# In the last hop TensorE turns the identity forty times a batch into an unused part of PSUM

## The chip, the cores and the metric

One core of one Trainium2 chip runs the kernel. The metric is the time on the device in microseconds, of the one core; lower is better.

## The reference

Two graph layers over 50,000 nodes of 128 features and 25,000 edges, each followed by a layer norm:

```python
x = layernorm(x + L0(x, (src, dst), edge_attr_70, Wf, bf, Wq, Wk, Wa, Wu, bu))
x = layernorm(x + L1(x, edge_attr3_4x1, src, dst))

# L0, per edge:  f = elu(concat(x[src], x[dst], x[src]-x[dst], attr) @ Wf + bf) * mask
#                a = tanh((x[src] @ Wq) * (f @ Wk) * scale @ Wa)
#                z = exp(a) / exp(segment_sum(a, src))[src] * f
#     result:    (x + segment_sum(z, src)) @ Wu + bu
# L1: e2 = e / segment_sum(e, dst)[dst] over the edges in both directions, self edges weigh 0
def f(y): return segment_sum(y[src3] * e3, dst3)       # four heads of 32 features
k1 = f(x); k2 = f(x + k1/3); k3 = f(x + k2 - k1/3); k4 = f(x + k1 - k2 + k3)
y = x + (k1 + 3*(k2 + k3) + k4) / 8
```

The second layer is linear in `f`, so the kernel applies `f` four times in a row ("four hops") and adds the results with the shares 1, 1/2, 1/6 and 1/24.

## The kernel before

The kernel sorts the 50,000 ends of edges by node, so that each of 128 partitions holds a run of 392 rows (`C`), worked in 49 batches (`NB`) of 8 rows (`B`). It has three parts, and each engine has its own program in each of them.

1. The edges' messages (0 to about 740 us), with the sort on VectorE.
2. The first layer's second pass (about 765 to 1450 us): GpSimd gathers message rows, VectorE sums runs and makes the norm's statistics, TensorE turns rows through the identity (line 831) and multiplies with `Wu` (lines 818 and 822).
3. The four hops (`hop(h)`, h = 0 to 3). For each batch GpSimd issues eight indirect gathers (line 1319); VectorE weighs the rows (`weigh`, line 1433, which raises `z_set`), adds the value carried over from the last row (`go_on`, 1444), sums runs with a scan in PSUM (`add_up_runs`, 1452), keeps the last row (`keep_last`, 1458, which raises `last_kept`) and divides (`divide`, 1462). ScalarE lays out the scan's pattern (1371) and scales the rows for the running total (1388), VectorE adds them (1417). SyncE moves totals and rows between HBM and SBUF.

In the hops 0 to 2 the nodes without edges are worked beside it: TensorE multiplies 384 of their rows a batch (`d_tensor`, line 1100), VectorE adds and makes statistics (`d_res_set` counts its additions), ScalarE scales.

The last hop (h = 3) also makes the output: VectorE adds the first layer's row to the total (`o_rows`, line 1185), takes the statistics with eight `bn_stats` (1189) and, after a wait on its own semaphore `o_stat`, eight `bn_aggr` (1193); ScalarE takes the root (`o_root`, 1161 and 1163) and scales eight rows (`o_scale`, 1170); GpSimd stores them with eight indirect DMAs (`o_put`, 1200). GpSimd's order there is: the gathers of batch b, then the stores of batch b - 4, which wait for `o_normed`. TensorE has nothing in the last hop's 49 batches. After the last batch it makes one product (`carry`, line 1353), which waits for `last_kept`; VectorE's `cross` (line 1527) waits for it, then `cross_sum` (1533), then the last batch's shift, which ScalarE's last `o_scale` and GpSimd's last eight stores need.

In PSUM the hops use banks 0 and 1 for the weighed rows (`z_all`), banks 2 to 4 for the weights (`wt`), bank 7 for the scaled rows (`shared`), columns 0 to 127 of bank 6 for the carry, and columns 128 to 511 of banks 5 and 6 for the dense products of the hops 0 to 2 (`d_new_psum`). In the last hop nothing uses bank 5.

Of the kernel before, what the change touches and what calls it, by code (L numbers as in the profile page):

```python
# [59 lines left out]
DC = N // 128 // DR  # L60
DMAIN = DC * DR * 128
DREST = N - DMAIN
DSLOTS = 44


def sort_before(k):
# [21 lines left out]
def build(nc, x, src, dst, e_in, Wf, bf, Wa, Wu, bu, x_t, ea_t, ea_0, wqk_in, out):  # L88
# [10 lines left out]
    with ExitStack() as ctx:  # L99
        def sb(name, shape, dt=F32, stage=None):  # L100
            return (stage or ctx).enter_context(nc.sbuf_tensor(name, shape, dt))
# [5 lines left out]
        bank = [psum[:, i * 512:(i + 1) * 512] for i in range(8)]  # L107

        ident = sb("ident", [128, 128])
# [949 lines left out]
        def d_landed(k):  # L1059
            return attr_count(NS - 1 - (NS - 1 - k) % 4) + times(k, 4) * 16  # L1060
# [6 lines left out]
        def d_shape(k):  # L1067
            return (DREST, 1) if k == DC else (128, DR)
# [14 lines left out]
        def d_store(sp, k):  # L1083
            if 0 <= k <= DC:
                P, RR = d_shape(k)
                sp.wait_ge(d_normed_set, k + 1)
                sp.dma_start(d_rows(out, k), d_normed[k % 4][0:P, 0:RR, :]).then_inc(d_out[k % 4], 16)

        def d_tensor(pe, k):
            if k > DC:  # L1090
                return
            P, RR = d_shape(k)
            if k == 0:
                pe.wait_ge(f_norm, 1)
                pe.wait_ge(wu_i_set, 1)
            pe.wait_ge(attr_in[k % 4], d_landed(k))
            if k >= 2:
                pe.wait_ge(d_res_set, k - 1)
            for r in range(RR):
                t = pe.matmul(d_new_psum[k % 2][0:P, r * D:(r + 1) * D], d_xt[k % 4][:, r * 128:r * 128 + P], wu_i[:, :],  # L1100
                              start=True, stop=True)
            t.then_inc(d_mm, 1)
# [115 lines left out]
        def hop(h):  # L1218
# [6 lines left out]
            def dense_at(b):  # L1225
                if h < 3 and 1 <= b <= (DC + 5 - 2 * DSLOTS if h == 2 else DSLOTS):
                    return h * DSLOTS + b - 1
                return None

            done = h * NB  # L1230
# [29 lines left out]
            def hop_sync(sp):  # L1260
# [5 lines left out]
                for b in range(NB + 1):  # L1266
# [13 lines left out]
                    if dense_at(b) is not None:  # L1280
                        d_store(sp, dense_at(b) - 5)
                    if h == 2 and b == DC + 6 - 2 * DSLOTS:
                        d_store(sp, DC)
# [64 lines left out]
            def hop_tensor(pe):  # L1348
                for b in range(NB):
                    if dense_at(b) is not None:  # L1350
                        d_tensor(pe, dense_at(b))
                pe.wait_ge(last_kept, (h + 1) * NPC)
                pe.matmul(carry, chain[:, :], last_z[:, 0:D], start=True, stop=True).then_inc(carried, 1)  # L1353

# [51 lines left out]
            def hop_vector(v):  # L1406
# [135 lines left out]
                if h == 3:  # L1542
# [11 lines left out]
                                           ).then_inc(f_norm, 1)  # L1554

            return hop_sync, hop_gpsimd, hop_tensor, hop_scalar, hop_vector

        hops = [hop(h) for h in range(4)]
# [69 lines left out]
```

## Time and profile before

| | |
|---|---|
| time, median of 3 runs | 4298.1 us (4269.28 to 4321.41) |
| the profiled execution's own time | 4300.45 us |
| its span in the trace | 4298.3 us |
| VectorE busy | 2368.8 us (55%), 6013 instructions |
| GpSimd busy | 2656.3 us (62%), 2760 instructions |
| ScalarE busy | 1326.2 us (31%) |
| TensorE busy | 879.6 us (20%), 3855 instructions |
| mean granted clock of TensorE | 0.575 of full speed |

An engine's busy time counts its instructions, not the time between them. For GpSimd that matters: each of its indirect DMAs is followed by about 0.3 us in which it issues the next one, and this time isn't in the 62%.

### The profile page before, as it was taken

How to read it: one execution, taken by the hardware profiler on the slowest of the kernel's cores; microseconds unless marked ns; L12 is line 12 of the kernel's file. 1: busy time of each engine (PE TensorE's matmuls, PEld its weight loads, DVE VectorE, ACT ScalarE, POOL GpSimd, SP SyncE). 2: the span in 40 equal slices, each digit the busy share in tenths (PEclk: the TensorE clock that was granted, in tenths of full speed). 3: DMA queues.
4: the chain of work that ended last, by engine and by line, in shares of the span. 5: the costliest groups of instructions: out<-in, count | busy, mean ns of one | idle time of the engine just before them, and what ended most of it. 6: DMA issues, size and time to landing. Idle time of an engine off the chain costs nothing.

```text
span 4298.3 us, 23047 instructions
## 1 busy us (share of the span) xinstructions
PE 879.6 (20%) x3855; PEld 697.7 (16%) x3855; DVE 2368.8 (55%) x6013; ACT 1326.2 (31%) x3061; POOL 2656.3 (62%) x2760
## 2 busy tenths in 40 slices
PE   2443545354555311110111110111100000000000
PEld 2443434133333201110011110111100000000000
DVE  5445441466666745665567765666765434443443
ACT  2332334254555312221233331333322222222222
POOL 5555553655555466665666656666657677666766
PEclk7776768677776655555555555555555555555555
DMA  4343337454555334443566665566653333332332
GB/s 88 115 130 109 128 104 147 131 161 156 158 161 157 113 104 126 128 134 117 173 217 224 223 209 177 194 226 211 226 181 127 111 97 113 110 101 92 127 98 86
DMA packets 272344, 621.66 MB, mean 145 GB/s; under 512 B 100374, under 2 KB 137199, under 8 KB 265945
## 3 DMA queue, kind: packets, MB, share of 16 engines
q1 hardware_dynamic: 176754, 421.49, 28.9%
q0 software_dynamic: 94672, 198.33, 17.0%
q14 instruction: 119, 0.97, 0.1%
q8 instruction: 31, 0.51, 0.0%
q10 hardware_dynamic: 768, 0.36, 0.0%
HBM read 318.61 MB, written 310.84 MB: 146 GB/s over the span
## 4 chain that ended last, share of the span: by engine, by line
DVE 26%; another core or an unknown queue 21%; issue 17%; POOL 10%; ACT 5%; PE 2%; DMA 1%; DVEq 0%; ACTq 0%; POOLq 0%
DVE psum L1452 8%; POOL gs L1319 5%; POOL out_dram L1200 4%; DVE da L1462 4%; PE psum L822 2%; ACT psum L1388 2%; DVE stats L933 2%; DVE psum L958 1%; DVE psum L1433 1%; DVE da L966 1%; DVE tn L1417 1%; DVE d_stats L1143 1%; DVE new_res L929 1%; DVE d_res L1138 1%
## 5 line engine op out<-in xcount | busy, mean ns | idle before, releaser
L1319 POOL DMA_INDIRECT gs<-u,far_row x1176 | 1120.5, 953 | 486.0 <-issue 347.6
L1388 ACT ACTIVATE psum<-da 128x512 f32<-128x512 f32 x288 | 173.2, 601 | 1612.7 <-remote 676.9
L318 POOL DMA_INDIRECT pt<-in_x_dram,idx x392 | 382.6, 976 | 321.7 <-DMA rows_e<-pt 198.8
L800 POOL DMA_INDIRECT gs<-rows_e,edge_id x392 | 371.6, 948 | 326.2 <-DVE new_res L929 155.8
L1200 POOL DMA_INDIRECT out_dram<-normed,out_idx x392 | 396.5, 1012 | 211.3 <-issue 115.5
L1100 PE MATMUL psum<-wu_i,d_xt 128*128 128x128 f32 (+1 forms) x782 | 211.0, 443 | 1421.9 <-DVE d_res L1138 501.7
L1319 POOL DMA_INDIRECT gs<-x1s,far_row x392 | 373.3, 952 | 175.7 <-issue 128.1
L1452 DVE TENSOR_TENSOR_SCAN psum<-goes_on,psum 128x1024 f32<-128x1024 f32 (+1 forms) x200 | 449.4, 2247 | 42.9 <-remote 23.7
L1100 PEld LDWEIGHTS psum<-wu_i,d_xt 128*128 128x128 f32 (+1 forms) x782 | 176.4, 326 | 1456.2 <-issue 1456.2
L1433 DVE TENSOR_TENSOR psum<-gs,psum 128x1024 f32<-128x1024 f32 x192 | 233.1, 1214 | 270.5 <-DMA gs<-u,far_row 228.4
L1417 DVE TENSOR_TENSOR tn<-psum,gs 128x512 f32<-128x512 f32 x288 | 197.7, 686 | 109.2 <-issue 66.5
L1353 PE MATMUL psum<-last_z,chain 128*128 128x128 f32 x8 | 3.2, 501 | 1173.0 <-issue 1073.8
L1462 DVE TENSOR_TENSOR da<-psum,inv 128x1024 f32<-128x1024 f32 (+1 forms) x200 | 238.6, 1193 | 0.3
L360 PE MATMUL psum<-w_src,xs_t 128*128 128x256 f32 x392 | 164.6, 511 | 348.9 <-ACT xd_t L390 277.0
L1371 ACT COPY goes_on<-cont_in 128x1024 f32<-128x1024 f32 (+1 forms) x200 | 201.9, 1011 | 68.1 <-DVE psum L1452 32.2
L1444 DVE SCALAR_TENSOR_TENSOR psum<-last_z,cont,psum 128x128 f32<-128x128 f32 x196 | 68.9, 352 | 271.8 <-remote 193.0
L664 DVE SCALAR_TENSOR_TENSOR act_f<-psum,ex 128x512 f32<-128x512 f32 x49 | 33.8, 690 | 334.6 <-ACT ex L440 202.1
L1353 PEld LDWEIGHTS psum<-last_z,chain 128*128 128x128 f32 x8 | 2.0, 311 | 1174.3 <-issue 1074.1
L822 PE MATMUL psum<-wu,rows_t 128*128 128x128 f32 x784 | 143.5, 357 | 222.9 <-ACT rows_t L886 160.8
L822 PEld LDWEIGHTS psum<-wu,rows_t 128*128 128x128 f32 x784 | 131.3, 261 | 278.0 <-ACT rows_t L886 205.3
L911 ACT ACTIVATE normed<-new_res,shift,rstd 128x128 f32<-128x128 f32 x392 | 156.2, 482 | 54.5 <-DVE shift L979 44.1
L929 DVE TENSOR_TENSOR new_res<-gs,psum 128x1024 f32<-128x1024 f32 (+1 forms) x50 | 60.0, 1199 | 190.9 <-PE psum L822 127.7
(223 smaller groups left out, 3036.1 us busy)
## 6 DMA issues: line engine op xcount, KB each, us to landing
u<-da SPq DMA_DIRECT2D x144, 512.0 KB
rows_e<-pt SPq DMA_DIRECT2D x48, 1056.0 KB
total<-tn SPq DMA_DIRECT2D x98, 512.0 KB
gs<-total SPq DMA_DIRECT2D x98, 512.0 KB
gs<-u SPq DMA_DIRECT2D x49, 512.0 KB
gs<-x1s SPq DMA_DIRECT2D x49, 512.0 KB
res_d<-new_res SPq DMA_DIRECT2D x49, 512.0 KB
d_xt<-x_t_dram SPq DMA_DIRECT2D x130, 192.0 KB
```

The source lines that it names most:

```text
L318: g.indirect_dma_start(pt[i][:, j, r, FX:FX + D], None, x[:, :], bass.IndirectOffsetOnAxis(ap=idx[:, r, s, j:j + 1], axis=0)).then_inc(x_i ...
L800: g.indirect_dma_start(gs[b % NG][:, j, :], None, rows_e[:, :], bass.IndirectOffsetOnAxis(ap=edge_id[:, c:c + 1], axis=0)).then_inc(x_in[b ...
L822: t = pe.matmul(new_psum[:, j * D:(j + 1) * D], xa_t[b % 2][:, j * 128:(j + 1) * 128], wu[:, :], start=False, stop=(j % 4 == 3))
L1100: t = pe.matmul(d_new_psum[k % 2][0:P, r * D:(r + 1) * D], d_xt[k % 4][:, r * 128:r * 128 + P], wu_i[:, :], start=True, stop=True)
L1200: g.indirect_dma_start(out[:, :], bass.IndirectOffsetOnAxis(ap=out_idx[:, c:c + 1], axis=0), normed[k % 3][:, j, :], None, bounds_check=bo ...
L1319: g.indirect_dma_start(gx[b % 4][:, j * D:(j + 1) * D], None, source[:, :], bass.IndirectOffsetOnAxis(ap=far_row[:, c:c + 1], axis=0)).the ...
L1371: act.copy(goes_on[i % 2][:, 0:n * D].rearrange("p (f j) -> p f j", j=n), cont_in[:, b * B + c0:b * B + c1].unsqueeze(1).to_broadcast([128 ...
L1388: act.mul(shared, half(us[b % 3], i), share).then_inc(shared_set, 1)
L1417: v.tensor_tensor(half(tn[b % 3][:, :, :], i), shared, half(tp[b % 3], i), ALU.add).then_inc(tn_set, 1)
L1433: return v.tensor_tensor(zf.rearrange("p (h f) j -> p j h f", h=H), by_head(gxv(b % 4)[:, c0:c1, 0:D]), per_head(wt_rest[:, c0:c1, :] if b ...
L1452: v.tensor_tensor_scan(z, goes_on[i % 2][:, 0:(c1 - c0) * D], z, 0.0, ALU.mult, ALU.add).then_inc(run_set, 1)
L1462: return v.tensor_tensor(by_head(us[b % 3][:, c0:c1, :]), zf.rearrange("p (h f) j -> p j h f", h=H), per_head(inv[:, b * B + c0:b * B + c1 ...
```

## The change

A constant `WARM` of 40, and six lines in TensorE's program for a hop. In the last hop, before the first batch, TensorE waits until VectorE has read the last dense product out of PSUM. Then, for each of the 49 batches, it waits until the batch's weighing product is done (`z_set`) and turns the 128x128 identity through itself forty times into columns 128 to 255 of bank 5. The carry's product stays behind the last of them in TensorE's queue. Nothing reads what is written, and no other engine's program changes.

```diff
--- before.py
+++ after.py
@@ -61,6 +61,7 @@
 DMAIN = DC * DR * 128
 DREST = N - DMAIN
 DSLOTS = 44
+WARM = 40
 
 
 def sort_before(k):
@@ -1349,6 +1350,12 @@
                 for b in range(NB):
                     if dense_at(b) is not None:
                         d_tensor(pe, dense_at(b))
+                    if h == 3:
+                        if b == 0:
+                            pe.wait_ge(d_res_set, DC + 1)
+                        pe.wait_ge(z_set, done + b + 1)
+                        for i in range(WARM):
+                            pe.transpose(bank[5][:, 128:256], ident[:, :], ident[:, :])
                 pe.wait_ge(last_kept, (h + 1) * NPC)
                 pe.matmul(carry, chain[:, :], last_z[:, 0:D], start=True, stop=True).then_inc(carried, 1)
```

## Rows read from the trace of the kernel before

**Rows 1.** Profile page: TensorE's busy tenths and granted clock in 40 slices, instruction queues

```profile
PE   2443545354555311110111110111100000000000
...
PEclk7776768677776655555555555555555555555555
...
q8 instruction: 31, 0.51, 0.0%
```

**Rows 2.** Windows: third and last hop; busy us (count) per engine, clock, DMA share, GB/s

```profile
2640.00:3188.00 548.00, 67.89 (x250) 56.36 (x250) 365.46 (x682) 170.99 (x365) 343.84 (x363) 0.50 0.63 207
3188.00:4298.30 1110.30, 0.80 (x2) 0.50 (x2) 493.65 (x1235) 273.04 (x637) 777.28 (x786) 0.50 0.33 108
```

**Rows 3.** Groups by line in the last hop: count, busy us, mean ns, idle before

```profile
L1200 POOL DMA_INDIRECT out_dram<-normed,out_idx x392 | 396.5, 1012 | 211.3 <-issue 115.5 <-ACT normed L1170 95.8
L1319 POOL DMA_INDIRECT gs<-u,far_row x392 | 378.8, 966 | 121.9 <-issue 118.9 <-DMA u<-cross,first_idx 2.7 <-remote 0.3
...
L1452 DVE TENSOR_TENSOR_SCAN psum<-goes_on,psum 128x1024 f32<-128x1024 f32 x48 | 109.8, 2288 | 10.9 <-remote 10.1 <-issue 0.8
...
L1193 DVE BATCH_NORM_AGGREGATE mv<-stats 128x2 f32<-128x6 f32 x392 | 33.8, 155 | 168.1 <-remote 120.3 <-issue 45.8
```

**Rows 4.** Timeline of one late stretch: start us, us, engine, line, count, idle before

```profile
3638.91 1.22 DVE L1185 SCALAR_TENSOR_TENSOR new_res<-gs,tn 128x1024 f32<-128x1024 f32 x1
...
3643.09 0.32 SPq L1279 DMA_DIRECT2D res_d<-new_res  x1
3643.09 1.65 DVE L1189 BATCH_NORM_STATS2 stats<-new_res 128x6 f32<-128x128 f32 x8 [2.96 <-remote]
...
3653.59 0.86 DVE L1193 BATCH_NORM_AGGREGATE mv<-stats 128x2 f32<-128x6 f32 x8 [8.86 <-issue]
...
3671.31 1.02 POOL L1200 DMA_INDIRECT out_dram<-normed,out_idx  x1 [6.17 <-ACT normed L1170]
```

**Rows 5.** Groups by line in the first layer's second pass, 820 to 1440 us

```profile
L800 POOL DMA_INDIRECT gs<-rows_e,edge_id x346 | 328.0, 948 | 257.9 <-DVE new_res L929 155.8 <-issue 102.1
...
L958 DVE TENSOR_TENSOR_SCAN psum<-goes_on,psum 128x1024 f32<-128x1024 f32 x45 | 103.3, 2295 | 39.0 <-remote 28.1 <-issue 8.0 <-DVE psum L954 2.0
...
L937 DVE BATCH_NORM_AGGREGATE mv<-stats 128x2 f32<-128x6 f32 x380 | 30.5, 153 | 1.7
```

**Rows 6.** Line 831 (turns through the identity): ns min/median/max, all its instructions

```profile
L831 PE MATMUL psum<-ident,da x392: 272/273/476, 772.0 to 1433.1; 128*128 128x128 f32 x196
```

**Rows 7.** Timeline of TensorE: eight turns of line 831, twice

```profile
1108.13 1.39 PE L831 MATMUL psum<-ident,da 128*128 128x128 f32 x8
...
1117.19 1.09 PE L831 MATMUL psum<-ident,da 128*128 128x128 f32 x8 [1.50 <-DVE da L966]
```

**Rows 8.** Timeline of the third hop: three dense products

```profile
2719.08 1.62 PE L1100 MATMUL psum<-wu_i,d_xt 128*128 128x128 f32 x6 [18.69 <-issue]
```

**Rows 9.** Groups by line in the third hop: the dense products

```profile
L1100 PE MATMUL psum<-wu_i,d_xt 128*128 128x128 f32 x246 | 66.4, 443 | 424.4 <-issue 182.9 <-DVE d_res L1138 131.8 <-remote 109.7
```

**Rows 10.** Timeline of the end: last product, carry, what waits for it, last stores

```profile
4247.77 0.70 DVE L1433 TENSOR_TENSOR psum<-gs,wt_rest 128x512 f32<-128x512 f32 x1
...
4254.87 0.29 DVE L1458 COPY last_z<-psum 128x128 f32<-128x128 f32 x1 [0.49 <-DVE psum L1452]
...
4255.59 0.80 PE L1353 MATMUL psum<-last_z,chain 128*128 128x128 f32 x2 [1073.84 <-issue]
...
4266.88 0.26 DVE L1527 TENSOR_TENSOR cross<-psum,inv_first 128x128 f32<-128x128 f32 x1
...
4275.19 3.19 ACT L1170 ACTIVATE normed<-new_res,shift,rstd 128x128 f32<-128x128 f32 x8 [0.59 <-remote]
...
4285.22 0.98 POOL L1200 DMA_INDIRECT out_dram<-normed,out_idx  x1 [0.31 <-issue]
...
4295.53 0.98 POOL L1342 DMA_INDIRECT out_dram<-new,fix_idx  x1 [0.30 <-issue]
```

## The prediction

> **What bounds the kernel now.** I read the page first, then windows by hop, then the groups by line in the last hop, then single stretches of the timeline. On the page TensorE's row is zero over the last quarter, and its granted clock stands at 0.5, the lower of its two levels (1.2 GHz), from about 1460 us to the end [rows 1]. The windows make the last hop 1110.3 us long, with VectorE busy 493.7 us, ScalarE 273.0 us, GpSimd 777.3 us, and the DMA engines at a third [rows 2]. None of these is full, but the groups by line show that GpSimd is the bound: its stores take 396.5 us and its gathers 378.8 us, between them lie 115.5 + 118.9 us in which it only issues the next one, and it waits 95.8 us for ScalarE's scaled rows and 3.0 us for other things. That is 396.5 + 378.8 + 115.5 + 118.9 + 95.8 + 3.0 = 1108.5 of the 1110.3 us [rows 2, 3]. So the last hop gets shorter only if the 95.8 us shrink or each indirect DMA gets cheaper, and longer if GpSimd waits more.
>
> Where do the 95.8 us come from? VectorE's eight bn_aggr, which need nothing but the eight bn_stats before them, sit idle 168.1 us in front of them over the hop [rows 3]. The timeline shows such a stretch. An addition ends at 3638.91 + 1.22 = 3640.13 us, yet both the statistics behind it on VectorE and SyncE's store of its result start only at 3643.09 us; then the first bn_aggr comes 8.86 us after the last bn_stats, and at 3671.31 us GpSimd has lost 6.17 us [rows 4]. I call this VectorE's lag: its completions are seen late. In the first layer's second pass the same pair of instructions has 1.7 us of idle time over 380 bn_aggr [rows 5]. That pass differs from the last hop in two ways. TensorE works there, with its clock often at the upper level (tenths 7 and 8 on the page) [rows 1]. And GpSimd rests: 155.8 us in waits for VectorE within 620 us [rows 5]. The trace of before can't part these two, and this is the main doubt of the forecast.
>
> **The change, part by part.** Nothing is removed or moved. Added in the last hop are:
>
> 1. One wait for the last dense addition. That addition belongs to the third hop, so the wait is over before the last hop has products. Cost nothing.
> 2. 49 waits on `z_set` in TensorE's program, and 49 x 40 = 1960 turns. Eight turns of line 831 take 1.09 us at best, the last of them being 0.27 us long, so the step is (1.09 - 0.27) / 7 = 0.117 us; another eight took 1.39 us, (1.39 - 0.27) / 7 = 0.16 us [rows 6, 7]. At the low clock no row has turns alone; the nearest are dense products in the third hop, six records in 1.62 us, one of them 0.443 us long, a step of (1.62 - 0.443) / 5 = 0.236 us [rows 8, 9]. I take a burst of forty between 40 x 0.117 = 4.7 us and 40 x 0.236 = 9.4 us, nearer 8 us, because TensorE has idled before each burst. If no turn overlapped the next, at the longest turn of 0.476 us, it would be 19.0 us [rows 6]. A batch lasts 1110.3 / 49 = 22.7 us [rows 2]. So a burst fits into its batch in each of these cases, TensorE is done before the next `z_set`, and the clock should rise within bursts. The work lies beside GpSimd's and costs nothing.
> 3. Instructions to fetch. The queue that I take for TensorE's, from its size of 0.51 MB for 3855 matmul and 3855 load records (66 bytes each), had 31 transfers [rows 1]. The change adds 3920, so 0.26 MB or 16 transfers, against 108 GB/s x 1110 us = 120 MB in the hop [rows 2]. Below: nothing. Above, if each stood in front of a gather for 1 us (an assumption; a gather instruction itself takes 0.97 us [rows 3]): 16 us. I take nothing, since gathers are issued up to three batches ahead.
> 4. The carry's product, which is now behind the last burst. The last product ends at 4247.77 + 0.70 = 4248.47 us. The burst then ends at 4248.5 + 9.4 = 4257.9 us, the carry 0.80 us later, at 4258.7 us instead of 4256.39 us. VectorE comes to `cross` only at 4266.88 us, so 8.2 us of cover remain; without that cover the cost would be 2.3 us. With 19.0 us for the burst the carry ends at 4268.3 us, 1.4 us after `cross` now starts. Behind it lies more cover: the last eight rows are scaled by 4275.19 + 3.19 = 4278.38 us and GpSimd stores them from 4285.22 us on, 6.8 us later [rows 10]. Cost nothing in both.
>
> Other engines' durations: does a working TensorE change them? VectorE's scan takes 2295 ns in the pass in which TensorE works and 2288 ns in the last hop, where it doesn't [rows 3, 5], and a gather 948 ns against 966 ns. So no row shows an instruction that gets slower or faster by more than 2% with TensorE's work beside it. The Trainium skill ("SBUF — State Buffer", section "Who interferes with whom") says that TensorE has SBUF ports of its own and that contention arises only at the pair that VectorE and GpSimd share. By that rule too the bursts cost nothing.
>
> Sum: 0 us against the profiled execution's 4300.45 us, which is 2.4 us above the median of 4298.1 us. I forecast 4298 us.
>
> **The rivals.**
>
> *VectorE's lag goes away (faster).* If that lag hangs on TensorE's idleness, as the comparison of the two stages allows, the bursts would make the last hop like the second pass, in which the pair has 1.7 us of idle time. GpSimd then no longer waits for scaled rows: at most 4300.45 - 95.8 = 4204.7 us, half of it 4252.6 us [rows 3, 5]. Against it: the dense products of the third hop keep TensorE busy 67.9 of 548 us [rows 2], and the pauses of GpSimd explain the clean stage as well. The Trainium skill ("TensorE: Matmul & The Clock Gate", section "Seeing it yourself") states that only TensorE has this clock gate, with none for VectorE. By that rule the raised clock gives the other engines nothing, and the sum stays at 4300; no run so far shows it.
>
> *VectorE's lag gets worse (slower).* In the last hop, between a product and the next, VectorE's completions are late already. If what delays them is a resource that all engines' instructions share, 80 more records a batch lengthen the lag. Each microsecond that it adds to GpSimd's wait is lost in full. Were the wait to double, the time is 4300.45 + 95.8 = 4396 us; from 43 us more on, an increase by 45%, the change is slower by 1% [rows 3]. Against it: the second pass runs TensorE, VectorE, ScalarE and GpSimd together with next to none of it [rows 5].
>
> *TensorE can't keep the pace.* From 22.7 / 40 = 0.57 us a turn on TensorE is the bound and the carry is late. At 0.70 us a burst takes 28 us, and 49 of them 1372 us, 262 us more than the hop, 4562 us. Against it: the longest of 392 turns took 0.476 us [rows 6].
>
> *The change doesn't do what it says:* the clock stays at 0.5. That costs and gains nothing, since bursts of 9.4 us are in the sum above. It shares the forecast's time.
>
> **How the numbers follow.** No change within 1%: 0.62, own range 4265 to 4330 us, about the spread of the three runs. Lag relieved: 0.22. Lag worse: 0.14. TensorE the bound: 0.02. One per cent is about what a measurement of this kernel can tell from no change. Of the relief's 0.22 I count 0.19 as more than 1%, and 0.02 of chance spread, so faster 0.21; slower 0.14 x 0.8 + 0.02 + 0.02 of spread = 0.15; the rest is 0.64. The range goes down to 4225 us, which leaves out the nearly full relief (about 0.10), and up to 4335 us, which leaves out about 0.09 of the slower cases.
>
> **What would show each step.** In the profile of after: 1960 turns at the new line with a burst of 5 to 9 us in each batch; the clock's row above 0.5 in the last quarter; GpSimd's wait for scaled rows still near 96 us, and the idle time before bn_aggr near 168 us; the carry's product later by 1 to 3 us with `cross` where it was. If the wait for scaled rows falls below 50 us, TensorE's idleness was the cause and I am wrong. If it rises above 140 us, the bursts stand in VectorE's way.

## The result, and the profile after

The changed kernel takes 4403.7 us (median of 4 runs, 4388.9 to 4414.4) beside 4304.8 us for the kernel before (4269.3 to 4321.4): a ratio of 1.022, 95% interval 1.018 to 1.026. That is outside the range given. The profiled execution took 4405.02 us, its span is 4403.2 us, 104.9 us more than the span before.

The page of the changed kernel, same rows as [rows 1] and TensorE's total:

```profile
PE 1211.6 (28%) x5815; PEld 955.4 (22%) x5815; DVE 2370.5 (54%) x6013; ACT 1326.3 (30%) x3061; POOL 2650.8 (60%) x2760
...
PE   2544433444455111110111101111032122211237
...
PEclk7777767677777555555555555555555555555568
...
q8 instruction: 46, 0.75, 0.1%
```

TensorE is at 1 to 3 tenths over the last quarter and at 7 only in the last slice. The clock's row stays at 0.5, the lower level (1.2 GHz), until the last two slices. So the turns are there, but thinly spread.

Groups by line in the last hop (count, busy us, mean ns, idle before and what ended it). The first two and the last answer to [rows 3]; line numbers are seven or fewer higher than before:

```profile
L1201 POOL DMA_INDIRECT out_dram<-normed,out_idx x392 | 395.9, 1010 | 311.2 <-ACT normed L1171 195.7 <-issue 115.5
L1320 POOL DMA_INDIRECT gs<-u,far_row x392 | 378.4, 965 | 121.9 <-issue 119.1 <-DMA u<-cross,first_idx 2.8
L1358 PE MATMUL psum<-ident 128*128 128x128 f32 x1960 | 354.5, 313 | 843.4 <-issue 823.1 <-DVE psum L1440 19.9
...
L1459 DVE TENSOR_TENSOR_SCAN psum<-goes_on,psum 128x1024 f32<-128x1024 f32 x48 | 109.9, 2289 | 10.6 <-remote 5.4 <-issue 4.7
```

GpSimd's own work is that of before, to within a microsecond. Its wait for scaled rows has gone from 95.8 to 195.7 us. And the 1960 turns have 843.4 us of idle time in front of them. 823.1 us of it end with nothing that the profile shows ("issue"), and only 19.9 us with the weighing product. The waits in the same stretch (engine, tile, line waited for: us in total, times, longest us):

```profile
POOL out_dram L1201 <- ACT normed L1171: 195.7, 13, 86.5
DVE mv L1194 <- remote: 152.9, 19, 9.6
...
DVE cross L1534 <- PE psum L1360: 103.1, 2, 102.8
ACT normed L1171 <- DVE shift L1177: 99.9, 1, 99.9
```

One single wait is 86.5 us long, so it makes most of the difference: VectorE's `cross` waits 102.8 us for the carry's product, the last shift comes behind it, and GpSimd's last eight stores behind that. The timeline shows how it comes about, first TensorE some 90 us into the hop (start us, us, engine, line, operation, count, idle before):

```profile
3285.45 0.37 PE L1358 MATMUL psum<-ident 128*128 128x128 f32 x1 [1.79 <-issue]
3288.26 0.37 PE L1358 MATMUL psum<-ident 128*128 128x128 f32 x1 [2.45 <-issue]
3291.07 0.37 PE L1358 MATMUL psum<-ident 128*128 128x128 f32 x1 [2.43 <-issue]
```

then a stretch in which GpSimd waits for scaled rows:

```profile
3249.78 14.76 PE L1358 MATMUL psum<-ident 128*128 128x128 f32 x110 [0.34 <-issue]
...
3256.10 1.02 POOL L1201 DMA_INDIRECT out_dram<-normed,out_idx  x1 [11.33 <-ACT normed L1171]
```

and the end, TensorE and GpSimd:

```profile
4302.65 0.98 POOL L1201 DMA_INDIRECT out_dram<-normed,out_idx  x1 [0.30 <-issue]
...
4306.28 79.44 PE L1358 MATMUL psum<-ident 128*128 128x128 f32 x711 [1.03 <-issue]
4385.56 0.39 PE L1360 MATMUL psum<-last_z,chain 128*128 128x128 f32 x2
...
4385.99 0.29 DVE L1534 TENSOR_TENSOR cross<-psum,inv_first 128x128 f32<-128x128 f32 x1 [102.78 <-PE psum L1360]
...
4390.18 1.00 POOL L1201 DMA_INDIRECT out_dram<-normed,out_idx  x1 [86.55 <-ACT normed L1171]
```

While GpSimd issues without a pause, a turn lasts 0.37 us and the next comes up to 2.80 us later. When GpSimd waits, TensorE catches up: GpSimd stands still from 3244.77 to 3256.10 us, and from 3249.78 us on 110 turns go in 14.76 us, 0.134 us each. Behind the first 53 turns the hop has ten such blocks, of 22 to 110 turns; each begins within one of the twelve waits for scaled rows that GpSimd has before its last. They hold 712 of the 1249 turns made until GpSimd stops, in 101.5 us; the 484 others take about 2.0 us each on average. When GpSimd issues its last store but eight, at 4302.65 us, more than 711 of the 1960 turns are undone, some 18 batches' worth. Some 2.7 us after that store has been issued, TensorE starts on these 711 and does them in 79.44 us, 0.112 us each, and only then comes the carry.

The sum of the difference: the hop starts 6.1 us later (its first gather at 3194.21 instead of 3188.10 us; up to there the two programs do the same, and in the traces of the experiments on such chips this gather starts anywhere from 3168.9 to 3213.8 us), the other waits for scaled rows grow from 95.8 to 195.7 - 86.5 = 109.2 us, 13.4 us more, and the late carry costs 86.5 us. Together that is 106.0 us, beside the 104.9 us of the two spans.

### The profile page after: what moved, and what is told of

Read it like the earlier page. It is cut to its first block, busy times and chain, and to the rows that moved or that the text cites. A ratio compares the mean times of both kernels' runs of the same rounds, so it can differ in the third digit from the quotient of the medians.

```text
span 4403.2 us, 26968 instructions
## 1 busy us (share of the span) xinstructions
PE 1211.6 (28%) x5815; PEld 955.4 (22%) x5815; DVE 2370.5 (54%) x6013; ACT 1326.3 (30%) x3061; POOL 2650.8 (60%) x2760
## 4 chain that ended last, share of the span: by engine, by line
issue 31%; DVE 24%; another core or an unknown queue 11%; PE 10%; POOL 3%; ACT 2%; DMA 1%; DVEq 0%; ACTq 0%; POOLq 0%
PE psum L1358 8%; DVE psum L1459 7%; DVE da L1469 4%; POOL gs L1320 2%; PE psum L823 2%; DVE psum L959 2%; DVE da L967 1%; DVE d_stats L1144 1%; DVE stats L934 1%; DVE psum L1440 1%; DVE tn L1424 1%; DVE new_res L930 1%; ACT psum L1395 1%; DVE d_res L1139 1%
## 5 line engine op out<-in xcount | busy, mean ns | idle before, releaser
L1358 PE MATMUL psum<-ident 128*128 128x128 f32 x1960 | 354.5, 313 | 843.4 <-issue 823.1
L1201 POOL DMA_INDIRECT out_dram<-normed,out_idx x392 | 395.9, 1010 | 311.2 <-ACT normed L1171 195.7
L1358 PEld LDWEIGHTS psum<-ident 128*128 128x128 f32 x1960 | 269.5, 161 | 928.5 <-issue 928.3
L1378 ACT COPY goes_on<-cont_in 128x1024 f32<-128x1024 f32 (+1 forms) x200 | 201.9, 1012 | 76.6 <-DVE psum L1459 50.8
L1171 ACT ACTIVATE normed<-new_res,shift,rstd 128x128 f32<-128x128 f32 x392 | 155.4, 479 | 99.9 <-DVE shift L1177 99.9
L912 ACT ACTIVATE normed<-new_res,shift,rstd 128x128 f32<-128x128 f32 x392 | 156.3, 482 | 50.5 <-DVE shift L980 47.7
```

The source lines that it names most:

```text
L1201: g.indirect_dma_start(out[:, :], bass.IndirectOffsetOnAxis(ap=out_idx[:, c:c + 1], axis=0), normed[k % 3][:, j, :], None, bounds_check=bo ...
L1358: pe.transpose(bank[5][:, 128:256], ident[:, :], ident[:, :])
```

## The experiments

**What was to be told apart.** Theory A: TensorE falls behind because each turn has to wait for something that all engines share while GpSimd issues without a pause; the forty turns a batch pile up and the carry is late. Rival B: the turns make VectorE's lag (its late completions) worse throughout the hop. Rival C: it is TensorE's own busy time, or the clock that follows from it.

### Turns in the first 28 batches only

```diff
-                    if h == 3:
+                    if h == 3 and b < 28:
```

> The forty turns stand only in the last hop's first 28 batches. Theory A, TensorE falls behind: in the changed kernel it has done about 31 bursts (1240 turns) when GpSimd stops at about 4300 us, so it gets through a turn in about 1090 / 1240 = 0.88 us while the hop runs. 28 bursts are 1120 turns, 985 us, done by 4192 us, before the last product; the carry's product is on time and the time is that of the kernel before, ratio 1.000 (within 1%). Theory B, the turns lengthen VectorE's lag and so GpSimd's waits all along the hop: 28 of 49 bursts keep 28/49 of the 99 us, about +57 us, ratio 1.013.

Measured: 4316.2 us, ratio 1.0028 (0.9995 to 1.0061). `cross` waits 0.3 us for TensorE, GpSimd 107.5 us for scaled rows, none of it over 11.4 us. The 1120 turns were all made in time, just fewer than the 1960 - 711 = 1249 that the changed kernel managed before GpSimd stopped. With no burst left in the queue the cost is gone but for 0.3%, which the interval doesn't tell from no cost. That is A; B would have kept more than half of it.

### Twenty turns, and eighty

```diff
-WARM = 40
+WARM = 20
```

> Twenty turns a batch in place of forty, in all 49 batches. Theory A: 980 turns at 0.88 us are 862 us of the hop's 1110, so TensorE is never more than a few batches behind and caught up at the end; ratio 1.000 to 1.005. Theory B: half the added instructions, half of the 99 us, about +50 us, ratio 1.012.

Measured: 4306.1 us, ratio 1.0048 (1.0011 to 1.0085). 49 x 20 = 980 turns are again below 1249, the carry's product is ready before `cross` needs it, and GpSimd waits 117.6 us in 15 waits of at most 11.7 us.

```diff
-WARM = 40
+WARM = 80
```

> Eighty turns a batch. Theory A: 3920 turns, of which about 1240 are done when GpSimd stops for want of scaled rows; the other 2680 run at 0.109 us each, 292 us, against 720 or 79 us in the changed kernel. So 214 us more than with forty turns, about 4618 us, with VectorE's cross waiting about 315 us. Theory B: twice the 99 us over the kernel before, about 4500 us, spread over the hop, with cross waiting little.

Measured: 4625.8 us, ratio 1.0774 (1.0739 to 1.0808), as A has it (4618 us). Repeated on another chip (below) it was 1.0775. The waits of the last hop and TensorE's timeline at its end:

```profile
POOL out_dram L1201 <- ACT normed L1171: 425.0, 15, 325.0
DVE cross L1534 <- PE psum L1360: 338.7, 1, 338.7
...
4292.38 317.98 PE L1358 MATMUL psum<-ident 128*128 128x128 f32 x2890 [0.34 <-issue]
4610.20 0.39 PE L1360 MATMUL psum<-last_z,chain 128*128 128x128 f32 x2
```

2890 turns were left when GpSimd stopped, so 3920 - 2890 = 1030 had been made; in the repeat it was 3920 - 2694 = 1226. With twice as many asked for, TensorE gets no more done beside GpSimd than the 1249 of the changed kernel. All that is asked beyond it stands at the end, at 0.110 us a turn.

### The same busy time in a quarter of the instructions

```diff
-WARM = 40
+WARM = 5
...
-                            pe.transpose(bank[5][:, 128:256], ident[:, :], ident[:, :])
+                            pe.matmul(bank[5][:, :], ident[:, :],
+                                      bu8[:, 0:4, :].rearrange("p j f -> p (j f)"), start=True, stop=True)
```

> Five products of the identity with 512 columns (10 load and 10 matmul records) a batch in place of forty turns (40 and 40), for about the same time of a busy TensorE (5 to 9 us a burst). Theory A, the number of TensorE's instructions sets how far it falls behind: 490 pairs in the hop instead of 1960, never behind, ratio 1.000 to 1.005. Theory C, a busy TensorE or its clock is what slows the hop: the same 99 us, ratio 1.023.

Measured: 4311.7 us, ratio 1.0043 (1.0011 to 1.0075). The group by line of the wide products, and TensorE's timeline some 100 us into the hop:

```profile
L1358 PE MATMUL psum<-bu,ident 128*128 128x512 f32 x490 | 316.7, 811 | 775.6 <-remote 413.9 <-issue 201.9 <-DVE psum L1441 159.9
...
3295.38 6.76 PE L1358 MATMUL psum<-bu,ident 128*128 128x512 f32 x10 [13.77 <-DVE psum L1441]
```

TensorE is busy 316.7 us beside the 354.5 us of the change, in 490 instructions where there were 1960 (each wide product is two), and it keeps the pace; `cross` doesn't wait for it. Its mean granted clock over the whole execution is higher too, 0.614 beside 0.594. So the number of instructions counts, and neither the busy time nor the clock does: C falls.

### Small turns, the last batch alone, and another chip

The next three kernels ran on a second chip, on which the kernel before takes 3573.2 us (19 runs, 3570.3 to 3578.1), and not 4299.4 us as in the four experiments above (21 runs, 4250.4 to 4330.4). First, turns of a sixteenth of the size, as many as in the change:

```diff
-                            pe.transpose(bank[5][:, 128:256], ident[:, :], ident[:, :])
+                            pe.transpose(bank[5][:, 128:144], ident[0:16, :], ident[0:16, 0:16])
```

> The same forty turns a batch, but each is of 16 columns of the identity into 16 columns of PSUM instead of 128 into 128, so that TensorE has as many instructions and far less to do in each. Theory A (a turn costs TensorE a slot, whatever is in it: 2.80 us while GpSimd issues without pause): the step of the turns stays near 2.8 us in the middle of the hop, some 18 bursts are left when GpSimd runs dry, the cross waits about 60 to 90 us for the carry's product, and the ratio is 1.015 to 1.022. The ends of that range differ by how fast the small turns go once GpSimd has stopped: 18 bursts of 40 at 0.109 us are 78 us, at half of that 39 us. Rival (a turn is held by its own work in TensorE or PSUM, so small ones keep up): cross waits under 3 us for TensorE and the ratio is 1.00 to 1.005.

Measured: ratio 0.9999 (0.9990 to 1.0009). By the expectation as written the rival had won. But neither theory had foreseen a chip without the thing in dispute, so this run tells nothing between them. Then forty turns behind the last batch's product alone:

```diff
-                    if h == 3:
+                    if h == 3 and b == NB - 1:
```

> Forty turns in the last of the 49 batches alone, ahead of the carry's product; the other 48 batches have none. Theory A: they start when that batch is weighed, some 25 us before GpSimd stops, take 2.80 us each until then (about 9) and 0.109 us each after (31, so 3.4 us); the carry's product ends 25 to 30 us later than before, which the stores still out hide for the most part: the ratio is 1.000 to 1.004, and the wait of the cross for TensorE is under 15 us. The small second cost of the other variants (10 to 20 us more in GpSimd's waits for scaled rows) must be gone, since 48 batches are those of before: 96 us, within 5. Rival (that second cost comes from the program's size or from the turns' place and not from turns taken in the middle): GpSimd waits 107 us or more, and the ratio is 1.003 to 1.005.

Measured: ratio 0.9998 (0.9988 to 1.0007). And a benchmark of the cost by itself, in which the whole computation is left out (its core):

```python
# GpSimd, a stretch each for 128 rows x 512 bytes, 128 x 64 bytes, 16 x 512 bytes, without pause
for i in range(K):
    g.indirect_dma_start(rows[0:P, i, 0:w], None, x[:, :], bass.IndirectOffsetOnAxis(
        ap=idx[0:P, i:i + 1], axis=0)).then_inc(traffic(name, i), 16)
# TensorE, behind the first of them
for i in range(TURNS):
    pe.transpose(psum[:, k * 512:k * 512 + 128], ident[:, :], ident[:, :])
# VectorE, at the same time: 24 small multiplications, each waits for the one before it
```

> The whole computation is left out. Seven stretches, one after the other: in each TensorE makes 36 of the change's turns back to back and VectorE 24 small multiplications, each waiting for the one before it, while one kind of other work is under way: nothing; GpSimd gathering 128 rows of 512 bytes by indirect transfers without pause; the same with rows of 64 bytes; the same with 16 rows of 512 bytes; SyncE storing 512 KB at a time in packets of 4 KB; SyncE storing in packets of 512 bytes; GpSimd computing and moving nothing. Theory A in three forms. A1 (it is GpSimd's issuing of indirect transfers): turns of about 2.8 us in all three gathering stretches, 0.1 to 0.25 us in the others. A2 (it is the number of packets): slow with 128 rows at both sizes and in the stretch of 512-byte stores, fast with 16 rows. A3 (it is bytes moved): slow in the two stretches of stores above all, fast at 64 bytes. Rival (it belongs to the kernel's own mix, such as engines that wait on each other): no stretch is slower than 0.476 us a turn.

Measured: all seven stretches at full pace, 36 turns beside the gathers in 5.63 us. Again a chip that has nothing to show; and 36 turns would have been too few on one that has, where 42 go at full pace first (below). So the question became whether the change itself costs anything here.

### The change itself on such a chip

> The changed kernel itself, beside the kernel before on this job's chip. The last job ran on a chip where the kernel before takes 3573 us and not 4299, and where its trace shows none of the slow steps: 392 gathers follow each other every 1.25 us there too, but VectorE has no lag and GpSimd waits for no scaled rows. Theory A (on the slower chip every engine's instructions share a path that falls behind while GpSimd issues without pause): on a chip of 4299 us the ratio is again 1.018 to 1.026; on one of 3573 us it is 1.000 within 0.002, because the 1960 turns hide at 0.109 us each. Rival (the cost belongs to the kernel and not to the chip): 1.02 on either.

Measured, on a third chip (before: 3578.9 us, 25 runs): 3578.0 us, ratio 0.9998 (0.9988 to 1.0007). Its last hop, by line, and its waits and timeline at the end:

```profile
L1201 POOL DMA_INDIRECT out_dram<-normed,out_idx x392 | 393.6, 1004 | 119.4 <-issue 119.4
L1358 PE MATMUL psum<-ident 128*128 128x128 f32 x1960 | 355.1, 368 | 616.9 <-DVE psum L1440 616.9
...
L1194 DVE BATCH_NORM_AGGREGATE mv<-stats 128x2 f32<-128x6 f32 x392 | 31.5, 153 | 1.7
...
3496.28 7.19 PE L1358 MATMUL psum<-ident 128*128 128x128 f32 x40 [13.30 <-DVE psum L1440]
3520.58 6.99 PE L1358 MATMUL psum<-ident 128*128 128x128 f32 x40 [17.11 <-DVE psum L1440]
3527.41 0.39 PE L1360 MATMUL psum<-last_z,chain 128*128 128x128 f32 x2
```

All idle time before the turns now ends with the weighing product, none with "issue". A burst takes 7.0 to 7.2 us of a batch of 20.5 us. GpSimd waits for no scaled row at all, and the idle time before `bn_aggr` is 1.7 us where it was 168.1 us [rows 3]: VectorE's lag isn't there either. The instructions last as long as on the other chip (a store 1004 ns and 1012 ns, a `bn_aggr` 153 ns and 155 ns); only the time between them differs. The two kinds of chip differ by 4299 - 3573 = 726 us in the kernel before, and one place where it sits can be read: on this chip the dense products of the first three hops have idle time that ends with nothing but VectorE's sums,

```profile
L1101 PE MATMUL psum<-wu_i,d_xt 128*128 128x128 f32 x780 | 210.3, 443 | 1168.9 <-DVE d_res L1139 1168.9
```

while on the chip of the trace before, in the third hop alone, 182.9 of 424.4 us ended with "issue" [rows 9]. On this chip the clock did rise, too. The page's row:

```profile
PEclk8787777888875555555555555555576666666666
```

It is at 0.6 and 0.7 where it is 0.5 in the kernel with forty turns behind the last batch alone on the same chip, and the time is the same; VectorE's scan takes 2285 ns in both. So a faster TensorE clock, by itself, gives this hop nothing. That is the rule of the Trainium skill ("TensorE: Matmul & The Clock Gate", section "Seeing it yourself") by which only TensorE has this gate; this trace agrees.

The other kernels on that chip, and the same again on a fourth one (before: 3574.2 us, 19 runs):

> The forty turns of a batch cut to 16 columns, as many instructions as in the change. On a chip of 3573 us: 1.000, as measured. On a chip of 4299 us, theory A (a turn costs a slot, whatever is in it): step near 2.8 us in the middle of the hop, cross waits 60 to 90 us for the carry's product, ratio 1.015 to 1.026. Rival (a turn's own work): ratio 1.000 to 1.005.

> Forty turns behind the last batch alone. On a chip of 3573 us: 1.000, as measured. On a chip of 4299 us, theory A: about 9 of them at 2.8 us until GpSimd stops and 31 at 0.109 us, the carry's product 25 to 30 us later than before, ratio 1.000 to 1.004, GpSimd's waits for scaled rows those of before (96 us within 5). Rival for the small second cost (program size or place of the turns): those waits 107 us or more and a ratio of 1.003 to 1.005.

> The whole computation is left out. As the benchmark before, with 150 turns in each stretch and earlier starts. On a chip of 3573 us: turns at 0.109 and 0.22 us in all seven stretches, the chain's steps the same in all. On a chip of 4299 us: A1 (GpSimd's issuing of indirect transfers fills the shared path): turns of about 2.8 us, after a start at full pace, in the three gathering stretches, not in the other four. A2 (number of packets): slow with 128 rows at both sizes and with stores in 512-byte packets, fast with 16 rows. A3 (bytes): slow in the stores above all. A4 (it takes several engines at once, not one issuer): fast in all seven.

> The forty turns of a batch cut to 16 columns. On a chip of 3573 to 3579 us: 1.000, as measured twice. On a chip of 4299 us, theory A (a turn costs a slot, whatever is in it): step near 2.8 us in the middle of the hop, cross waits 60 to 90 us for the carry's product, ratio 1.015 to 1.026. Rival (a turn's own work): ratio 1.000 to 1.005.

> Forty turns behind the last batch alone. On a chip of 3573 to 3579 us: 1.000, as measured twice. On a chip of 4299 us, theory A: about 9 of them at 2.8 us until GpSimd stops and 31 at 0.109 us, the carry's product 25 to 30 us later than before, ratio 1.000 to 1.004, GpSimd's waits for scaled rows those of before (96 us within 5). Rival for the small second cost (program size or place of the turns): those waits 107 us or more and a ratio of 1.003 to 1.005.

> As the benchmark with 150 turns in each stretch, once more, in the hope of a chip on which the kernel before takes 4299 us (two jobs in a row fell on one of 3573 to 3579 us, where every stretch went at full pace, as expected there). On a chip of 4299 us: A1 (GpSimd's issuing of indirect transfers fills the shared path): turns of about 2.8 us, after a start at full pace, in the three gathering stretches, not in the other four. A2 (number of packets): slow with 128 rows at both sizes and with stores in 512-byte packets, fast with 16 rows. A3 (bytes): slow in the stores above all. A4 (it takes several engines at once, not one issuer): fast in all seven.

Measured: the small turns 0.9997 (0.9988 to 1.0007) and 1.0003 (0.9992 to 1.0013); the last batch alone 1.0000 (0.9991 to 1.0010) and 0.9998 (0.9988 to 1.0008). In the benchmark with 150 turns a stretch, those beside the gathers of 128 rows x 512 bytes took 18.24 and 18.02 us, 0.12 us a turn. On three chips of about 3575 us nothing costs anything.

### The benchmark where the kernel before takes 4281 us

> The benchmark of 150 turns a stretch once more, as the last two calls fell on chips of 3573 to 3579 us (full pace in every stretch, chain and turns alike). On a chip of 4299 us: A1 (GpSimd's issuing of indirect transfers): turns of about 2.8 us, after a start at full pace, in the three gathering stretches and not in the other four. A2 (number of packets): slow with 128 rows at both sizes and with stores in 512-byte packets, fast with 16 rows. A3 (bytes): slow in the stores above all. A4 (it takes several engines at once): fast in all seven.

Measured on a fifth chip (before: 4280.9 us, 3 runs). TensorE's timeline in the stretch of 128 rows x 512 bytes (PEld is the load of the identity, PE the product; the two make one turn):

```profile
98.65 6.40 PE L126 MATMUL psum<-ident 128*128 128x128 f32 x42 [77.58 <-DMA rows<-in_x_dram,idx]
106.00 0.14 PEld L126 LDWEIGHTS psum<-ident 128*128 128x128 f32 x1 [1.18 <-issue]
107.39 0.27 PE L126 MATMUL psum<-ident 128*128 128x128 f32 x1 [2.34 <-issue]
108.80 0.18 PEld L126 LDWEIGHTS psum<-ident 128*128 128x128 f32 x1 [2.66 <-issue]
110.20 0.37 PE L126 MATMUL psum<-ident 128*128 128x128 f32 x1 [2.53 <-issue]
```

and its windows, one for each kind of traffic: 128 rows x 512 bytes, 128 x 64 bytes, 16 x 512 bytes, then SyncE's stores in packets of 4 KB and of 512 bytes (the last window takes in 30 iotas of the stretch behind it; us, then busy us and count of each engine, clock, DMA share, GB/s):

```profile
98.00:298.00 200.00, 39.59 (x150) 25.81 (x150) 4.81 (x25) 124.13 (x132) 0.52 0.15 43
375.00:560.00 185.00, 38.51 (x150) 23.35 (x150) 5.23 (x25) 123.89 (x131) 0.53 0.06 6
630.00:835.00 205.00, 39.54 (x150) 25.34 (x150) 4.57 (x25) 130.26 (x132) 0.52 0.02 5
855.00:885.00 30.00, 18.80 (x150) 18.60 (x150) 4.25 (x25) 0.00 (x0) 0.78 1.02 405
935.00:965.00 30.00, 18.73 (x150) 18.52 (x150) 4.25 (x25) 5.49 (x30) 0.78 1.04 286
```

The very pattern of the kernel, with nothing of the kernel left in it. After 42 turns at full pace (66 in the stretch of 64-byte rows) TensorE starts one instruction every 1.40 us, load and product in turn, so the step of the turns is mostly 2.80 us, and 150 turns need 185 to 205 us. It is as slow with 16 rows as with 128, at 64 bytes as at 512, at 5 GB/s as at 43. It is absent beside SyncE's stores at 405 and at 286 GB/s. So it is neither the bytes nor the packets (A2 and A3 fall) nor the mix of engines (A4 falls); it is what GpSimd issues (A1). VectorE's chain was hit in the same way in two of the three stretches of gathers: 17 of its 24 links came at 0.23 to 0.24 us, the rest 0.7 to 2.1 us apart. In the stretch of 64-byte rows all 24 went at full pace.

Eighty turns on the same chip:

> Eighty turns a batch instead of forty. On the chip of 4299 us this gave 1.077, as theory A had it (2.80 us a turn while GpSimd issues without pause). On a chip of 3573 to 3579 us a turn has its own step of 0.109 us, 80 of them are 8.7 us of a batch of 20.4 us, and TensorE keeps the pace: ratio 1.000 within 0.003, the last burst's 80 turns put the carry's product 8.7 us later than before, and the cross waits for it under 3 us. Rival (a turn costs time on such a chip too, and forty are just too few to show it): a ratio of 1.01 or more and waits of GpSimd for scaled rows that the kernel before doesn't have there.

Measured: 4607.9 us, ratio 1.0775 (1.0701 to 1.0850), `cross` waiting 321.7 us. The cost of this kind of chip repeats on a second chip of it.

### With pauses, and with GpSimd computing

Only the pause between groups of gathers is changed; last come 900 iotas without a DMA:

```python
if i % every == every - 1 and i < K - 1:      # every = K, 20, 8, 4
    g.wait_ge(tl[name], min(i + 1, LEAD) * 16)
    if i >= LEAD:
        g.wait_ge(tr[name], (i + 1 - LEAD) * 16)
```

> The whole computation is left out. Stretches as in the benchmark with 150 turns, but now GpSimd's gathers of 128 rows of 512 bytes differ in their pauses only: none, then a wait for everything that is out behind every 20, every 8 and every 4 of them (a wait of about 2 us each, the time a gather takes to land), and last 900 short iotas without a DMA. On a chip where the kernel before takes 3573 to 3579 us: full pace everywhere. On one of 4281 to 4299 us: theory P (GpSimd's issue without a pause keeps the others' path full, and a pause lets it drain): the turns are at 2.80 us between the pauses and some go at 0.109 us in each pause, so that the 150 turns take about 200 us with no pause, less with every 20, and under 60 us with every 4; the iotas leave the turns at full pace. Rival N (only the number of indirect transfers counts): each of the gathering stretches slows turns alike, by about 2.8 us a turn while gathers are issued, pauses or not. Rival G (any instruction of GpSimd does it): the iotas' stretch is slow too.

Measured on the same chip (before: 4288.5 us, 12 runs). Windows of the five stretches, no pause, every 20, every 8, every 4, iotas:

```profile
98.00:236.00 138.00, 31.95 (x150) 22.96 (x150) 5.10 (x25) 81.11 (x87) 0.56 0.14 41
306.00:442.00 136.00, 31.42 (x150) 22.70 (x150) 4.77 (x25) 82.50 (x88) 0.56 0.15 42
513.00:540.00 27.00, 19.56 (x148) 19.19 (x149) 4.78 (x25) 17.58 (x19) 0.77 0.15 44
730.00:755.00 25.00, 18.28 (x150) 18.17 (x150) 4.97 (x25) 14.59 (x16) 0.79 0.14 39
885.00:955.00 70.00, 19.24 (x150) 19.04 (x150) 4.39 (x25) 68.55 (x799) 0.62 0.01 2
```

The longest blocks at full pace in them, one line of TensorE's timeline for the pauses of every 20, 8 and 4 and for the iotas:

```profile
306.89 6.46 PE L129 MATMUL psum<-ident 128*128 128x128 f32 x42 [79.91 <-DMA rows<-in_x_dram,idx]
...
519.37 15.14 PE L129 MATMUL psum<-ident 128*128 128x128 f32 x110 [87.29 <-DMA rows<-in_x_dram,idx]
...
736.72 18.38 PE L129 MATMUL psum<-ident 128*128 128x128 f32 x150 [196.30 <-DMA rows<-in_x_dram,idx]
...
902.19 19.24 PE L129 MATMUL psum<-ident 128*128 128x128 f32 x150 [147.10 <-POOL many L88]
```

The iotas, one every 0.086 us, leave the turns alone: rival G falls. With a pause of about 2 us behind every 8 gathers the 150 turns are free but for three gaps, with one behind every 4 entirely; one behind every 20 does nothing. Rival N falls, and P was right that a pause matters, though not in its sizes: without a pause it wanted 200 us and 128 were measured, as the 80 gathers behind the first 60 last only 100 us, and for "every 20" it had hoped for a gain. With the pauses counted in, one gather every 1.25 or 1.32 us slows the turns, and one every 1.47 us (every 8) hardly does. (The 140 gathers of a stretch start within 173.7, 183.8, 204.1 and 234.0 us, so a mean of 1.25, 1.32, 1.47 and 1.68 us.) If it is the mean that counts, the bound lies between 1.32 and 1.47 us; it may as well be the number of gathers in an unbroken row, between 8 and 20, for both changed together.

The last kernel, forty turns behind the last batch alone:

> Forty turns behind the last batch alone. On a chip of 3573 to 3579 us: 1.000, as measured three times. On one of 4281 to 4299 us, theory A: about 9 of them at 2.8 us until GpSimd stops and 31 at 0.109 us, the carry's product 25 to 30 us later than before, ratio 1.000 to 1.004, GpSimd's waits for scaled rows those of before (96 us within 5). Rival for the small second cost (program size or place of the turns): those waits 107 us or more and a ratio of 1.003 to 1.005.

Measured: 4280.8 us, ratio 0.9985 (0.9955 to 1.0016), GpSimd's waits for scaled rows 95.0 us (expected 96 within 5). Its time is that of before: the place at the end is free.

With turns in the middle of the hop a small second cost is left, even when TensorE is done in time. From the first gather to the end of the span the last hop takes 1110.2 us before and 1109.3 us with forty turns behind the last batch alone, but 1123.6 us with the first 28 batches, 1131.3 us with twenty turns and 1121.5 us with the wide products. That agrees with their ratios of 1.0028, 1.0048 and 1.0043, of which only the last two are clear of 1. The waits for scaled rows explain it only in part: the three have 107.5, 117.6 and 100.2 us, and in the two runs with eighty turns a batch these waits, without the long one at the end, are 100.0 and 105.8 us. Each number is from a single trace, so that this cost comes from the turns in the middle is likely, but not shown for each of them.

One detail of A was not met: none of the forty took 2.80 us. TensorE's two lines, and GpSimd's at the same time:

```profile
4246.01 6.93 PE L1358 MATMUL psum<-ident 128*128 128x128 f32 x40 [1077.42 <-remote]
4252.77 0.39 PE L1360 MATMUL psum<-last_z,chain 128*128 128x128 f32 x2
...
4249.10 0.99 POOL L1201 DMA_INDIRECT out_dram<-normed,out_idx  x1 [8.54 <-ACT normed L1171]
```

Two things fit, and no run parts them: the benchmark's 42 free turns, since nothing of TensorE had gone before these forty; and GpSimd's wait of 8.54 us from 4240.56 to 4249.10 us, in which they began, as the blocks at full pace in the changed kernel do.

**What stays open.** What the path is: that there is one, which fills and drains, is argued from the free turns at the start and after pauses, and isn't seen itself. On the chips of 4300 us, instructions of TensorE and VectorE are held back (in the benchmark to one every 0.7, 1.4 or 2.1 us) while GpSimd issues an indirect DMA every 1.25 to 1.3 us; on those of 3575 us they aren't, with the same instructions and durations. The Trainium skill ("NOTIFIC — the notification-queue block", sections "Overflow: three behaviours, one of which stalls the engine" and "Constraints, capacities, measured rates") describes one candidate: the block that writes the engines' trace records can hold about 500 of them, and when it is full it holds back the engines that produce them. The same page says that a record costs the engine nothing, which on the chips of 4300 us would then not be so. No run here tests it, since every execution timed here was also recorded. Whether the cost exists in an execution without records was not tried, nor whether direct DMAs issued by GpSimd cost the same as indirect ones. That the small turns go as slowly as large ones on a chip of 4300 us was not measured either, since those three runs were on chips of the other kind.

## Why the prediction was wrong, point by point

- **What bounds the kernel.** Right. GpSimd's 777.3 us of work and 234.4 us of issue are unchanged, and all that the hop lost is in its waits.
- **Part 1, the wait for the last dense addition.** Right, nothing: the first turn waits for the weighing product.
- **Part 2, the turns. This is the step that failed.** It priced a burst by the steps of turns inside one record, 0.117 to 0.236 us, took the longest turn, 0.476 us, as the worst case, and said that a burst fits "in each of these cases". The turns themselves last what it said (mean 313 ns). But their step in the hop is up to 2.80 us while GpSimd issues, and 1249 turns took the 4306.28 - 3194.21 = 1112 us until GpSimd stopped, 0.89 us each on average, where 0.57 us was the limit that the prediction itself gave. A sign of it stood in the rows. The dense products at the low clock, from which the 0.236 us came, have 18.69 us of idle time ended by "issue" in front of them [rows 8], and the whole group 182.9 us of it [rows 9]. Most of such a gap is an ordinary wait. What these products needed was VectorE's addition in the same trace:

```profile
2715.46 0.55 DVE L1138 TENSOR_TENSOR d_res<-bu,psum 128x384 f32<-128x384 f32 x1
```

It ended at 2716.01 us, and TensorE began at 2719.08 us, within 0.11 us of VectorE's own statistics of that addition: 3.1 us in which both waited for nothing visible. I read the step from inside the record and not the gap before it. And the rows for the warm turns were from the second pass, where GpSimd rests 155.8 us [rows 5]; that was named as the main doubt, but for VectorE alone. What holds VectorE's instructions back for nothing that the profile shows holds TensorE's too.
- **Part 3, instruction fetch.** Right: 46 - 31 = 15 transfers more where 16 were expected, and no gather is longer (965 ns, 966 before).
- **Part 4, the carry behind the last burst.** The chain of events was right: carry, `cross`, last shift, last stores, with up to 8.2 us of cover. The term was mis-sized. It counted one burst in front of the carry, 9.4 to 19.0 us, and there were 18, 79.4 us and more (the 711 turns left are 17.8 bursts); the carry came at 4385.56 instead of 4258.7 us. It had to follow from part 2: who falls behind by a little in each batch pays for it all at the end.
- **Other engines' durations.** Right: the scan takes 2289 ns (2288 before), a store 1010 (1012). What the engines do to each other shows in the gaps between instructions, not in their lengths.
- **Rival, lag relieved (0.22).** Fell. The lag isn't tied to TensorE's idleness: it goes on beside busy turns (the idle time before `bn_aggr` is 194.6 us with them and 168.1 us without), and on the chip without it, it is absent with and without turns.
- **Rival, lag worse (0.14).** It named the kind of resource that theory A supposes, one that "all engines' instructions share", and the wrong victim. The effect that it speaks of is at most 13.4 us in this trace, a seventh of the 95.8 us that it needed to reach 4396 us. That the time of 4404 us is near its number is chance: it came by another road.
- **Rival, TensorE can't keep the pace (0.02).** This is what happened. The chance was far too low, since the only row held against it was the length of a turn. Its time of 4562 us took 0.70 us a turn to the end; in fact the pace is worse (0.89 us) until GpSimd stops, and 0.11 us after it.
- **The markers.** 1960 turns: yes. Bursts of 5 to 9 us: some, in GpSimd's waits, but others take up to 94 us. The clock's row above 0.5: in the last two slices only. Carry later by 1 to 3 us: 4385.56 - 4255.59 = 130 us. Wait for scaled rows above 140 us: yes, and the text beside it ("the bursts stand in VectorE's way") holds only for the end.
- **On a chip of 3575 us** the steps of the sum held: bursts of 7.2 us, inside the 4.7 to 9.4 us given, and a ratio of 0.9998.

## What to carry to other kernels

Before you hide work on an idle engine, look not only at how long its few instructions in that stretch last, but also at when they start: compare it with the end of what they needed. "Issue" alone doesn't tell, for it can hide an ordinary wait, but a start microseconds after everything was ready is a warning. While GpSimd issued without a pause, such a delay came back here for turn after turn. Count instructions, not busy time, when another engine issues indirect DMAs without a pause; ten wide ones a batch kept the pace where forty narrow ones piled up. And put nothing that may fall behind in front of a product that the end of the kernel waits for: forty turns behind the last batch alone cost nothing, the same forty in each batch cost 86.5 us in a single wait. Lastly, compare with the kernel before on the same chip: its time differed by a fifth between chips, and the change cost 2.2% on one kind and nothing on the other.

## What the runs showed of the hardware

- Two kinds of chip. The same program takes 3573 to 3579 us on three of them and 4281 to 4299 us on two others, with equal durations of its instructions and unequal gaps between them.
- On the second kind, indirect DMAs issued by GpSimd every 1.25 us hold TensorE's instructions (load and product) to one every 1.40 us, so a turn to 2.80 us, after 42 to 66 turns at full pace. With 16 or 128 rows, 64 or 512 bytes each, 5 or 43 GB/s, the 150 turns take 185 to 205 us beside 192 such DMAs; beside SyncE's stores at 405 GB/s they go at full pace, and so they do beside an iota every 0.086 us. Pauses behind every 8 of the DMAs, a mean of one every 1.47 us, lift it.
- In the kernel GpSimd's own waits do the same: in ten of twelve, of 6.2 to 11.3 us, a block of 22 to 110 turns at full pace begins.
- Forty turns of the identity take 6.0 to 7.4 us after a rest, in which they start at the lower clock (granted 0.50 at the start of a burst of the change on a chip of 3579 us, 0.96 at its end), and 40 x 79.44 / 711 = 4.5 us in a long row of them.
